# The first stage of a six-stage decoder kernel: decays beside the convolution, halves of the products added on GpSimd, root scale and out projection per step inside the mixing loop

## The chip, the cores and the metric

The kernel runs on one core of one Trainium2 chip. The time is the device time of one launch in microseconds (us). The kernel before takes 1787.82 us (median of 3 runs, 1786.68 to 1789.52). Engines are named as in the profile: PE is TensorE (PEld its weight loads), DVE is VectorE, ACT is ScalarE, POOL is GpSimd, SP is SyncE.

## What is computed

Two decoder layers over x of 8 sequences x 128 positions x 512 features. The change is in the first of six stages alone. That stage is a bottleneck of 512 to 128 features, two passes through one "hydra" block (a two-way state space mixer that runs over the 8 sequences as its time axis, with the 128 positions as batch), and the way back up:

```
hidden = gelu(x @ w_down.T + b_down)
for each of 2 layers:                       # u starts as hidden
    zxbcdt = u @ in_w.T                     # z 256 | xBC 288 | dt 8
    xBC = silu(causal_conv(xBC, 7 taps) + conv_b);  xs, B, C = split(xBC)
    dt_fw, dt_bw = softplus(dt + dt_bias)
    y = scan forward (shifted by one) + scan backward (shifted by one)
    y = y + xs * (xs @ fcD_w.T + D)
    yz = y * silu(z)
    u = (yz * rsqrt(mean(yz^2) + 1e-5) * norm_w) @ out_w.T
x = layernorm(2 x + up(mix of u and hidden) ...)
```

The scan over 8 steps is not run step by step. It is written as an 8 x 8 table of weights for each position and each of 4 heads, so that y of step t is the sum over the 8 source steps s of weight(t, s) times xs(s). Everything is float32.

## The kernel before, in words

All of it is written out by hand: each engine has its own program in `hydra_stage`, and semaphores order them. What stands first in an engine's program runs first there. A position is a partition (128), a step t is one of the 8 sequences (`L` = 8).

The stage begins with the loads, the down projection on PE (L256) and Gelu on ACT (L325). The context for the next stage is loaded into the same buffer as soon as the down projection has read it (L210), and POOL splits it in high and low parts in eight instructions, `cT_hi` and `cT_lo` (L243, L245). Then each layer goes through five parts, in a loop of two rounds on every engine:

1. z and convolution: for each t one matmul for z and dt (L268), then 1 to 7 taps of two passes each for the convolution (L275). ACT takes z out (L336, L337), DVE adds the bias (L382), ACT does Silu (L339).
2. Transposes of xs (L284) and the skip weights (L289) on PE. Beside them a chain of small instructions on DVE: softplus (L386 to L400), the sums of dt over distances (L405, L407), the exponents (L408, L411), Exp on ACT (L347), and the table of mixing weights `mixw` (L414 to L435).
3. The mixing loop: for each t DVE forms `prod` = xs times weight for all 8 sources (L442, 128 x 2048), PE adds the 8 sources with 8 matmuls by the identity (L298), DVE multiplies by silu(z) into `yz` (L448), ACT takes the square sum (L352). `prod` has two buffers.
4. After the loop, for all t together: the mean square (L450), its power of -1/2 on POOL (`rms`, L248), the scaling of `yz` (L453).
5. Transposes of `yz` (L306), the copy to `yT` with norm_w as scale (L356), the out projection with 512 columns (L311), and the copy to `uT` (L360), on which the next layer's first matmul waits.

At the end DVE forms `xtok` = 2 x + b_up (L456), the mix with the hidden (L461, L462), PE the up projection (L319), and DVE adds (L466).

## Time and profile before

| | |
|---|---|
| median of 3 runs | 1787.82 us |
| profiled execution, its own time | 1786.91 us |
| span of the trace in it | 1785.1 us |
| first stage, from the start to the last `xtok` addition | 204.6 us of the span |
| PE busy | 1564.1 us (88%) |
| DVE busy | 961.3 us (54%) |
| ACT busy | 769.7 us (43%) |
| POOL busy | 696.7 us (39%) |
| granted clock of PE, mean | 0.94 |

The busy shares are means over six stages that have different limits. For this change only the first 205 us count, and in them which engine waits for which, so the rows further down come from views of that stretch, and a few from a later stage where POOL and DVE work at the same time.

In a row of the timeline the two first numbers are the start and the duration in us, then come engine, line, operation, output<-input, the shapes, how many instructions the row merges, and in brackets the idle time before it with what ended it.

### The profile page before, as it was taken

To read this page: it belongs to the slowest core of one execution; us is meant where nothing else is said; L and a number is where in the kernel's file an instruction comes from. 1 tells how busy PE (TensorE), PEld (TensorE's weight loads), DVE (VectorE), ACT (ScalarE), POOL (GpSimd) and SP (SyncE) were. 2 spreads that over 40 slices of the span, in tenths; PEclk is the share of its full clock that TensorE was granted. 3 is DMA by queue.
4 is the path that set the end of the run, shared out by engine and by line. 5 is a ranking of instruction groups with operands and counts; after the bars stand their busy time and mean duration, and the time that the engine had idled before them with its cause. 6 is when DMAs were issued, how large, how long until landed. Compare 5 with 4: busy or idle time off the path is not lost. (4 is left out here: it accounts for less than half of the span.)

```text
span 1785.1 us, 28858 instructions
## 1 busy us (share of the span) xinstructions
PE 1564.1 (88%) x10647; PEld 1282.0 (72%) x10647; DVE 961.3 (54%) x1673; ACT 769.7 (43%) x2389; POOL 696.7 (39%) x561
## 2 busy tenths in 40 slices
PE   5888799999996789885899648999999999999846
PEld 3767597888885566665677437888888888888734
DVE  0627611333355889884466824555555555556644
ACT  2131223444443333332899824455455445445400
POOL 4100113443421455552533535555554555542210
PEclk9888899999998899997999878999999999999968
DMA  5100100100101342305000131101101110000011
GB/s 195 36 0 0 36 18 19 37 20 21 49 2 36 130 165 83 118 1 148 1 2 14 36 98 58 36 24 37 47 15 47 37 36 25 24 1 1 1 42 47
DMA packets 63475, 77.75 MB, mean 44 GB/s; under 512 B 13884, under 2 KB 43052, under 8 KB 63340
## 3 DMA queue, kind: packets, MB, share of 16 engines
q1 hardware_dynamic: 60860, 74.36, 13.2%
q8 instruction: 84, 1.38, 0.3%
q0 software_dynamic: 464, 1.32, 0.3%
q10 hardware_dynamic: 2016, 0.27, 0.1%
q14 instruction: 51, 0.42, 0.1%
HBM read 73.85 MB, written 2.10 MB: 43 GB/s over the span
## 5 line engine op out<-in xcount | busy, mean ns | idle before, releaser
L989 POOL TENSOR_TENSOR xa_rs<-xa_ms,minus_half 128x5 f32<-128x5 f32 x64 | 74.9, 1171 | 168.7 <-DVE xa_ms L1211 168.7
L1469 DVE SCALAR_TENSOR_TENSOR ff_acc<-ff_ring,ff_sT,ff_acc 128x512 f32<-128x512 f32 x168 | 125.5, 749 | 25.4 <-ACT ff_acc L1429 13.7
L972 POOL TENSOR_TENSOR xa_prob<-xa_prob,xa_inv 128x512 f32<-128x512 f32 x64 | 66.7, 1042 | 138.0 <-DVE xa_inv L1178 138.0
L1379 PE MATMUL ff_ring<-xT_hi,ff_w 128*128 128x512 f32 x224 | 96.5, 431 | 27.2 <-ACT ff_acc L1429 12.1
L1156 ACT ACTIVATE xa_prob<-xa_prob,xa_peak 128x128 f32<-128x128 f32 x256 | 99.8, 391 | 42.5 <-DVE xa_peak L1222 42.5
L1206 DVE TENSOR_REDUCE xa_ssq<-xa_qn 128x4 f32<-128x512 f32 x64 | 43.9, 686 | 135.2 <-ACT xa_qn L1142 135.2
L605 POOL TENSOR_TENSOR xa_prob<-xa_prob,xa_inv 128x1024 f32<-128x1024 f32 x32 | 60.7, 1897 | 142.2 <-DVE xa_inv L859 142.2
L71 PE MATMUL xa_qp<-xa_q_hi,xT_hi 128*128 128x512 f32 x256 | 107.4, 420 | 2.4 <-DVE xa_q_lo L1169 2.4
L71 PE MATMUL xa_rows<-xa_o_hi,xa_out_hi 128*128 128x512 f32 x256 | 102.6, 401 | 5.2 <-DVE xtok L1185 5.2
L1847 ACT ACTIVATE sa_work<-sa_work,sa_peak 128x128 f32<-128x128 f32 x256 | 99.2, 394 | 10.0 <-DVE sa_peak L1884 9.9
L73 PE MATMUL xa_rows<-xa_o_lo,xa_out_hi 128*128 128x512 f32 x256 | 102.9, 402 | 0.0
L72 PE MATMUL xa_rows<-xa_o_hi,xa_out_lo 128*128 128x512 f32 x256 | 102.6, 401 | 0.0
L72 PE MATMUL xa_qp<-xa_q_hi,xT_lo 128*128 128x512 f32 x256 | 101.9, 398 | 0.0
L73 PE MATMUL xa_qp<-xa_q_lo,xT_hi 128*128 128x512 f32 x256 | 101.4, 396 | 0.0
L841 DVE TENSOR_REDUCE xa_peak<-xa_score 128x4 f32<-128x1024 f32 x32 | 39.2, 1224 | 115.6 <-PE xa_score L683 115.6
L1142 ACT ACTIVATE xa_qn<-xa_qp 128x512 f32<-128x512 f32 x64 | 38.2, 597 | 141.6 <-PE xa_qp L73 141.6
L1681 POOL TENSOR_TENSOR sa_work<-sa_work,sa_inv 128x1024 f32<-128x1024 f32 x32 | 60.8, 1899 | 92.2 <-DVE sa_inv L1888 92.1
L1380 PE MATMUL ff_ring<-xT_lo,ff_w 128*128 128x512 f32 x224 | 91.7, 410 | 0.0
L71 PE MATMUL xa_kvp<-xa_kv_hi,cT_hi 128*128 128x256 f32 x256 | 78.2, 305 | 8.6 <-DVE xa_kv_lo L1164 8.6
L1379 PEld LDWEIGHTS ff_ring<-xT_hi,ff_w 128*128 128x128 f32 x224 | 44.2, 197 | 55.0 <-DVE ff_acc L1469 22.4
L73 PE MATMUL xa_kvp<-xa_kv_lo,cT_hi 128*128 128x256 f32 x256 | 72.5, 283 | 0.0
L72 PE MATMUL xa_kvp<-xa_kv_hi,cT_lo 128*128 128x256 f32 x256 | 72.5, 283 | 0.0
(389 smaller groups left out, 4786.5 us busy)
## 6 DMA issues: line engine op xcount, KB each, us to landing
xa_raw_q<-in_wq SPq DMA_DIRECT2D x8, 1024.0 KB, 5.5
xa_raw_o<-in_wo SPq DMA_DIRECT2D x8, 1024.0 KB, 5.4
ff_dn_q<-in_down_w SPq DMA_DIRECT2D x7, 512.0 KB, 3.7
ff_dn_z<-in_down_z SPq DMA_DIRECT2D x7, 512.0 KB, 4.7
ff_dn_s<-in_down_s SPq DMA_DIRECT2D x7, 512.0 KB, 6.4
pre<-in_wq SPq DMA_DIRECT2D x16, 192.0 KB, 3.2
pre<-in_wo SPq DMA_DIRECT2D x16, 192.0 KB, 4.0
sa_work<-in_w_qkvT SPq DMA_DIRECT2D x3, 1024.0 KB, 8.6
```

Source lines behind the costliest of these rows:

```text
L71: pe.matmul(out, a_hi, b_hi, start=first, stop=False)
L72: pe.matmul(out, a_lo, b_hi, start=False, stop=False)
L73: return pe.matmul(out, a_hi, b_lo, start=False, stop=last)
L605: pool.tensor_tensor(prob[:, t % 3, :, :], prob[:, t % 3, :, :], bc(inv[:, t % 3, :], 2, [P, Q, KEYS]), ALU.mult).then_inc(s["norm"], 1)
L972: pool.tensor_tensor(prob[:, u % 2, :, :], prob[:, u % 2, :, :], bc(inv[:, u % 2, :], 2, [P, Q, S]), ALU.mult).then_inc(s["norm"], 1)
L989: pool.tensor_tensor(rs[:, :], ms[:, :], m.minus_half[:, 0:Q + 1], ALU.pow).then_inc(s["rs"], 1)
L1156: last = act.activation(prob[:, u % 2, h, :], prob[:, u % 2, h, :], ACT.Exp, bias=peak[:, u % 2, h:h + 1], accum_out=total[:, u % 2, h:h + 1])
L1379: pe.matmul(bank[:, :], w[:, g % 2, c, a, f], m.xT_hi[:, c, cols], start=True, stop=False)
L1380: pe.matmul(bank[:, :], w[:, g % 2, c, a, f], m.xT_lo[:, c, cols], start=False, stop=True).then_inc(s["grp"], 1)
L1469: dve.scalar_tensor_tensor(acc[:, n % 2, i // 4, :], ring[(8 * n + i) % RING][:, :], column(n, i), acc[:, n % 2, i // 4, :], ALU.mult, ALU ...
L1681: pool.tensor_tensor(prob[:, u % 3, :, :], prob[:, u % 3, :, :], bc(inv[:, u % 3, :], 2, [P, HC, S]), ALU.mult).then_inc(s["norm"], 1)
L1847: last = act.activation(prob[:, t % 3, h, :], prob[:, t % 3, h, :], ACT.Exp, bias=peak[:, t % 3, h:h + 1], accum_out=total[:, t % 3, h:h + 1])
```

## The change

- **Loads.** `w_down` and `b_down` are loaded first, x in two halves of 512 columns; the first half of the down projection waits for its half alone.
- **Layer 1 reads the Gelu output itself** (`x_mid`) and no copy of it.
- **Order of z and convolution.** All 8 z matmuls come first, then the convolutions, which have four banks instead of two; the transposes of xs and the skip weights are put between the convolutions of later steps.
- **Decays beside the convolution.** On DVE the softplus, the distances, the exponents and the multiplication by dt stand between the bias additions. `xtok` = 2 x + b_up moves there too, in layer 1.
- **Halves on GpSimd.** POOL adds the upper four sources of `prod` to the lower four, in place (128 x 1024), and PE adds four sources instead of eight. `prod` has three buffers.
- **Per step inside the mixing loop.** The mean square, the root on POOL (128 x 1), the transposes of `yz` (now not scaled), the out projection with positions as rows (128 columns), the scaling by `rms` when ACT takes that out, a transpose back and the copy to `uT` are done for each t. norm_w is multiplied into `w_out` once. The separate scaling of `yz` is gone.
- The loops over the two layers are written out. The multiplication of `x_mid` by the mix factor moves to the start of layer 2.

The core of the diff:

```diff
-        prod = [sb(f"prod{i}", [P, L, DIN]) for i in range(2)]
-        yz = sb("yz", [P, L, DIN])
+        PRODS, GATED = 3, 4
...
+        prod = [sb(f"prod{i}", [P, L, DIN]) for i in range(PRODS)]
+        yz = sb("yz", [P, GATED, DIN])
...
+                def halves(n, t):
+                    pool.wait_ge(s["prod"], n + 1)
+                    x = prod[n % PRODS]
+                    pool.tensor_tensor(x[:, 0:L // 2, :], x[:, 0:L // 2, :], x[:, L // 2:L, :], ALU.add).then_inc(s["half"], 1)
+
+                def root(n, t):
+                    pool.wait_ge(s["msq"], n + 1)
+                    pool.tensor_tensor(rms[:, t:t + 1], msq[:, t:t + 1], m.minus_half[:, 0:1], ALU.pow).then_inc(s["rms"], 1)
...
-                with pool.Fori(0, LAYERS) as i:
-                    pool.wait_ge(s["msq"], i + 1)
-                    pool.tensor_tensor(rms[:, :], msq[:, :], m.minus_half[:, 0:L], ALU.pow).then_inc(s["rms"], 1)
+                for i in range(LAYERS):
+                    for t in range(L + 3):
+                        if t < L:
+                            halves(L * i + t, t)
+                        if t >= 3:
+                            root(L * i + t - 3, t - 3)
...
+                def mixed_sum(i, t):
+                    n = L * i + t
+                    pe.wait_ge(s["half"], n + 1)
+                    if t >= 2:
+                        pe.wait_ge(s["yz"], n - 1)
+                    for src in range(L // 2):
+                        last = pe.matmul(bank[2 + t % 2][:, 0:DIN], m.ident[:, :], prod[n % PRODS][:, src, :], start=src == 0, stop=src == L // 2 - 1)
+                    last.then_inc(s["y_mm"], 1)
...
+                    for t in range(L + 4):
+                        if t < L:
+                            mixed_sum(i, t)
+                        if 2 <= t < L + 2:
+                            turn_y(i, t - 2)
+                        if 3 <= t < L + 3:
+                            project_out(i, t - 3)
+                        if t >= 4:
+                            turn_u(i, t - 4)
...
+                    softplus_in(i)
+                    conv_bias(i, 0)
+                    conv_bias(i, 1)
+                    softplus_out(i)
+                    conv_bias(i, 2)
+                    conv_bias(i, 3)
+                    conv_bias(i, 4)
+                    distances()
+                    conv_bias(i, 5)
+                    exponents()
+                    if i == 0:
+                        dve.wait_ge(ld["up"], 48)
+                        dve.scalar_tensor_tensor(m.xtok[:, :, :], m.xtok[:, :, :], 2.0, bc(b_up[:, :], 1, [P, B, D]),
+                                                 ALU.mult, ALU.add).then_inc(s["xres"], 1)
+                    conv_bias(i, 6)
+                    decays(i)
+                    conv_bias(i, 7)
+                    mixing_weights(i)
+                    for t in range(L + 3):
+                        if t < L:
+                            products(i, t)
+                        if 2 <= t < L + 2:
+                            gated(i, t - 2)
+                        if t >= 3:
+                            mean_square(i, t - 3)
```

Where instructions stand before and after, at three places. First POOL, from the last split of the context to the end of the stage, before (L245 is `cT_lo`, L248 the root for all 8 steps):

```order
L245 TENSOR_TENSOR cT_lo<-pre,cT_hi 128x1024
L246 UNCONDITIONAL_BRANCH
L246 ISA
L248 TENSOR_TENSOR hy_rms<-hy_msq,minus_half 128x8
L246 REGISTER_ALU
L246 COMPARE_AND_BRANCH
```

and of the change, the first layer (L261 is `cT_lo`, L230 the addition of the halves, L234 the root of one step):

```order
L261 TENSOR_TENSOR cT_lo<-pre,cT_hi 128x1024
L230 TENSOR_TENSOR hy_prod<-hy_prod 128x1024 x4
L234 TENSOR_TENSOR hy_rms<-hy_msq,minus_half 128x1
L230 TENSOR_TENSOR hy_prod<-hy_prod 128x1024
L234 TENSOR_TENSOR hy_rms<-hy_msq,minus_half 128x1
L230 TENSOR_TENSOR hy_prod<-hy_prod 128x1024
```

POOL, which had one instruction per layer here, has sixteen, and none of them can start before its eight instructions for the context are done.

Second DVE, at the end of the convolution of the first layer, before (L382 is the bias addition of step 7, L386 to L397 the begin of softplus, L63 counts a semaphore's value):

```order
L382 TENSOR_TENSOR hy_xbc<-hy_bank,hy_conv_b 128x288
L386 TENSOR_TENSOR hy_sp<-hy_dt_raw,hy_dt_bias 128x64
L63 ISA
L389 SCALAR_TENSOR_TENSOR hy_sp<-hy_sp 128x64
L390 REGISTER_ALU
L391 TENSOR_SCALAR hy_sp<-hy_sp 128x64
```

and of the change, the same instructions among the bias additions (L454):

```order
L458 TENSOR_TENSOR hy_sp<-hy_dt_raw,hy_dt_bias 128x64
L461 SCALAR_TENSOR_TENSOR hy_sp<-hy_sp 128x64
L454 TENSOR_TENSOR hy_xbc<-hy_bank,hy_conv_b 128x288 x2
L465 TENSOR_SCALAR hy_sp<-hy_sp 128x64
L466 RECIPROCAL hy_sp<-hy_sp 128x64
L467 TENSOR_TENSOR hy_sp<-hy_sp 128x64
L468 TENSOR_TENSOR hy_sp<-hy_sp 128x64
L469 TENSOR_SCALAR hy_sp<-hy_sp 128x64
L471 SCALAR_TENSOR_TENSOR hy_sp<-hy_sp 128x64 x6
L472 SCALAR_TENSOR_TENSOR hy_sp<-hy_sp 128x64
L473 TENSOR_SCALAR hy_sp<-hy_sp 128x64
L474 SCALAR_TENSOR_TENSOR hy_dt<-hy_sp 128x64
```

The whole softplus now stands after the bias addition of step 1 and ahead of that of step 2 (the next row is L454 x3, steps 2 to 4).

Third DVE in the mixing loop, before (L442 products, L448 `yz`):

```order
L442 TENSOR_TENSOR hy_prod<-hy_xbc,hy_mixw 128x2048 x2
L448 TENSOR_TENSOR hy_yz<-hy_bank,hy_z_act 128x256
L442 TENSOR_TENSOR hy_prod<-hy_xbc,hy_mixw 128x2048
L448 TENSOR_TENSOR hy_yz<-hy_bank,hy_z_act 128x256
L442 TENSOR_TENSOR hy_prod<-hy_xbc,hy_mixw 128x2048
```

and of the change (L521 products, L532 `yz`, L536 the mean square of one step):

```order
L521 TENSOR_TENSOR hy_prod<-hy_xbc,hy_mixw 128x2048 x3
L532 TENSOR_TENSOR hy_yz<-hy_bank,hy_z_act 128x256
L521 TENSOR_TENSOR hy_prod<-hy_xbc,hy_mixw 128x2048
L532 TENSOR_TENSOR hy_yz<-hy_bank,hy_z_act 128x256
L536 TENSOR_SCALAR hy_msq<-hy_ssq 128x1
L521 TENSOR_TENSOR hy_prod<-hy_xbc,hy_mixw 128x2048
```

The products run one step further ahead of `yz`, and the mean square of each step is taken between them.

## Rows read from the trace of the kernel before

**Rows 1.** Windows: us, busy of PE, PEld, DVE, ACT, POOL, then PEclk, DMA, GB/s

```profile
53.20:70.30 17.10, 13.24 (x52) 11.54 (x53) 14.82 (x49) 3.25 (x9) 0.00 (x0) 0.50 0.27 91
70.30:97.00 26.70, 26.17 (x122) 22.69 (x120) 16.59 (x14) 3.60 (x15) 0.00 (x0) 1.00 0.00 1
101.00:111.20 10.20, 9.04 (x19) 4.08 (x20) 0.66 (x3) 4.52 (x15) 0.00 (x0) 0.50 0.00 0
111.20:138.50 27.30, 23.58 (x101) 17.70 (x99) 6.05 (x18) 11.46 (x34) 0.00 (x0) 1.00 0.00 0
```

**Rows 2.** Timeline of the mixing loop of the first layer, one step

```profile
79.24 0.42 DVE L448 TENSOR_TENSOR hy_yz<-hy_bank,hy_z_act 128x256 f32<-128x256 f32 x1 [0.83 <-PE hy_bank L298]
79.58 2.28 DVE L442 TENSOR_TENSOR hy_prod<-hy_xbc,hy_mixw 128x2048 f32<-128x2048 f32 x1
```

**Rows 3.** Timeline from the first layer's last square sum to the second layer's first matmul

```profile
97.76 1.68 POOL L248 TENSOR_TENSOR hy_rms<-hy_msq,minus_half 128x8 f32<-128x8 f32 x1 [45.73 <-DVE hy_msq L450]
99.47 2.19 DVE L453 TENSOR_SCALAR hy_yz<-hy_yz,hy_rms 128x256 f32<-128x256 f32 x8 [1.79 <-POOL hy_rms L248]
...
112.86 0.71 PE L268 MATMUL hy_bank<-hy_w_zdt,hy_uT 128*128 128x264 f32 x2 [0.69 <-ACT hy_uT L360]
```

**Rows 4.** Timeline before the loops: both layers' first products, the second layer's first `mixw` step

```profile
64.60 4.49 DVE L442 TENSOR_TENSOR hy_prod<-hy_xbc,hy_mixw 128x2048 f32<-128x2048 f32 x2
...
142.82 1.22 DVE L414 TENSOR_TENSOR hy_cb_prod<-hy_xbc 128x1024 f32<-128x1024 f32 x1
...
147.60 4.49 DVE L442 TENSOR_TENSOR hy_prod<-hy_xbc,hy_mixw 128x2048 f32<-128x2048 f32 x2
```

**Rows 5.** Timelines of POOL and DVE at four places where they meet

```profile
49.67 2.36 POOL L245 TENSOR_TENSOR cT_lo<-pre,cT_hi 128x1024 fp32r<-128x1024 f32 x1
50.52 0.46 DVE L382 TENSOR_TENSOR hy_xbc<-hy_bank,hy_conv_b 128x288 f32<-128x288 f32 x1 [3.38 <-PE hy_bank L275]
50.89 1.21 DVE L386 TENSOR_TENSOR hy_sp<-hy_dt_raw,hy_dt_bias 128x64 f32<-128x64 f32 x1
...
134.07 0.21 DVE L386 TENSOR_TENSOR hy_sp<-hy_dt_raw,hy_dt_bias 128x64 f32<-128x64 f32 x1
...
601.81 1.28 POOL L1337 TENSOR_TENSOR cT_lo<-ff_acc,cT_hi 128x512 fp32r<-128x512 f32 x1 [0.74 <-ACT cT_hi L1436]
601.92 1.72 DVE L1503 TENSOR_TENSOR ff_w<-ff_other 128x512 fp32r<-128x512 int32 x1
...
612.30 1.22 DVE L1476 TENSOR_TENSOR ff_dn_w<-ff_dn_q,ff_dn_z 128x1024 f32<-128x1024 int32 x1
612.53 2.15 POOL L1343 TENSOR_TENSOR ff_acc<-ff_acc 128x512 f32<-128x512 f32 x1 [3.06 <-DVE ff_acc L1469]
```

**Rows 6.** Lines, two of them: durations min/median/max in ns of DVE L1487 and POOL L1343

```profile
L1487 DVE TENSOR_TENSOR ff_w<-pre x4: 684/685/692, 574.0 to 575.8; 128x512 fp32r<-128x512 int32 x4
...
L1343 POOL TENSOR_TENSOR ff_acc<-ff_acc x28: 1281/1301/2146, 590.8 to 796.2; 128x512 f32<-128x512 f32 x28
```

**Rows 7.** Groups by line and shape, POOL, whole span: busy us, mean ns of one

```profile
L1546 POOL TENSOR_TENSOR rstd<-var,minus_half 128x1 f32<-128x1 f32 x32 | 19.2, 600 | 89.6 <-DVE var L1541 89.6
...
L245 POOL TENSOR_TENSOR cT_lo<-pre,cT_hi 128x1024 fp32r<-128x1024 f32 x4 | 9.4, 2357 | 0.3
```

**Rows 8.** Timeline of PE, first layer: a convolution of 7 taps and the skip weights

```profile
46.92 3.56 PE L275 MATMUL hy_bank<-hy_w_conv,hy_uT 128*128 128x288 f32 x14
...
56.77 6.83 PE L289 MATMUL hy_skip_bank<-hy_fcd,hy_xsT 128*128 128x4 f32 x32
```

**Rows 9.** Timeline: the down projection, w_conv, the first z, the context's split

```profile
17.01 9.83 PE L256 MATMUL hy_bank<-pre,hy_w_down 128*128 128x512 f32 x16 [17.01 <-DMA hy_b_down<-in_b_down]
17.67 4.44 POOL L239 TENSOR_TENSOR hy_w_conv<-hy_taps,hy_w_xbc 128x2016 f32<-128x2016 f32 x1 [9.44 <-DMA hy_w_xbc<-in_in_wT]
...
31.52 0.38 ACT L336 ACTIVATE hy_z_act<-hy_bank 128x256 f32<-128x256 f32 x1
...
34.83 1.89 POOL L243 TENSOR_TENSOR cT_hi<-pre,ones 128x1024 fp32r<-128x1024 f32 x1 [12.72 <-DMA pre<-in_ctxT]
```

More of the change, by code:

```diff
@@ new lines, in conv @@
+                def conv(i, t):
+                    u = uT if i else x_mid
+                    if t >= 4:
+                        pe.wait_ge(s["c_out"], L * i + t - 3)
+                    first = max(0, TAPS - 1 - t)
+                    for k in range(first, TAPS):
+                        last = pe.matmul(bank[2 + t % 4][:, 0:CONV], u[:, token(t - (TAPS - 1) + k)], w_conv[:, k, :],
+                                         start=k == first, stop=k == TAPS - 1)
+                    last.then_inc(s["c_mm"], 1)
@@ new lines, in turn_xs, with skip @@
+                def turn_xs(i, t):
+                    n = L * i + t
+                    pe.wait_ge(s["xbc"], n + 1)
+                    pe.wait_ge(s["z_out"], L * i + L)
+                    if t >= 2:
+                        pe.wait_ge(s["xs_T"], n - 1)
+                    for c in range(2):
+                        last = pe.transpose(bank[t % 2][:, c * P:(c + 1) * P], xbc[:, t, c * P:(c + 1) * P], m.ident[:, :])
+                    last.then_inc(s["xs_tr"], 1)
+                def skip(i, t):
+                    pe.wait_ge(s["xs_T"], L * i + t + 1)
+                    for c in range(2):
+                        last = pe.matmul(skip_bank[:, t * NH:(t + 1) * NH], xsT[:, c, token(t)], fcd[:, c, :], start=c == 0, stop=c == 1)
+                    last.then_inc(s["skip"], 1)
@@ new lines, in project_out, with turn_u @@
+                def project_out(i, t):
+                    n = L * i + t
+                    pe.wait_ge(s["y_T"], n + 1)
+                    if t >= 2:
+                        pe.wait_ge(s["u"], n - 1)
+                    for c in range(2):
+                        last = pe.matmul(bank[t % 2][:, 0:DM], yT[:, t % 2, c, :], w_out[:, c, :], start=c == 0, stop=c == 1)
+                    last.then_inc(s["o_mm"], 1)
+                def turn_u(i, t):
+                    n = L * i + t
+                    pe.wait_ge(s["o_out"], n + 1)
+                    pe.transpose(bank[t % 2][:, DM:2 * DM], u_tok[:, t % 2, :], m.ident[:, :]).then_inc(s["u_tr"], 1)
@@ L332, in _ @@
                 act.activation(neg_a[:, :], a_log[:, :], ACT.Exp).then_inc(s["a_exp"], 1)
-                with act.Fori(0, LAYERS) as i:
+                for i in range(LAYERS):
                     for t in range(L):
@@ new lines, in _ @@
+                        if t == 5:
+                            act.wait_ge(s["seg"], i + 1)
+                            act.activation(dec[:, :, :, :, :], dec[:, :, :, :, :], ACT.Exp).then_inc(s["dec"], 1)
+                        if t >= 2:
+                            out_xsT(i, t - 2)
+                    for t in range(L - 2, L):
+                        out_xsT(i, t)
+                    for t in range(2, L + 4):
+                        if t < L + 2:
+                            square(i, t - 2)
+                            out_yT(i, t - 2)
+                        if 3 <= t < L + 3:
+                            out_rows(i, t - 3)
+                        if t >= 4:
+                            out_uT(i, t - 4)
@@ new lines, in _ @@
+                dve.memset(seg[:, :, :, :, :], 0.0).then_inc(s["pool"], 1)
+                dve.wait_ge(ld["small"], 16 * 9)
+                dve.tensor_scalar(a_log[:, :], a_log[:, :], A_LOG_CEIL, None, ALU.min).then_inc(s["na"], 1)
+                for c in range(2):
+                    dve.tensor_scalar(w_out[:, c, :], w_out[:, c, :], norm_w[:, c:c + 1], None, ALU.mult).then_inc(s["w_out"], 1)
+                dve.wait_ge(s["alpha_exp"], 1)
+                pre = Chain(dve, s["alpha"])
+                pre.step(dve.tensor_scalar(sp[2][:, 0:1], sp[0][:, 0:1], 1.0, None, ALU.add))
```

263 lines of the change are left out of this document (130 added, 133 removed).

## The prediction, as it went on record before the changed kernel ran

> **What bounds the stage now.** I read the page first: PE is busy for 88% of the span, but that is a mean over six stages. So I took the windows of the first 205 us, then the timeline of that stretch, then groups by line and shape for prices, and last the timelines of POOL and DVE in a later stage, where both work at once.
>
> In the mixing loop PE is busy for 26.17 of 26.70 us at the full granted clock, 2.4 GHz [rows 1], and each step DVE waits 0.83 us for PE [rows 2]. A step takes 0.83 + 0.42 + 2.28 less an overlap of 0.08, 3.45 us, for 16 passes of PE: 0.216 us a pass. PE sets the loop.
>
> Outside the loop nothing is bound by an engine; it is a row of handovers. I cut the stage in five stretches. Start to the first product: 64.60 us. First product of layer 1 to the first matmul of layer 2: 64.60 to 112.86, 48.3 us [rows 3, 4]. Of this the loop takes 33.2 (to 97.76) and what stands behind it 15.1 (root 1.68, scaling 2.19, transposes, projection). From there to the second first product: 147.60 - 112.86 = 34.7 us. Layer 2's loop I take as the first one's, 48.3. The rest is the up projection, some 9 us.
>
> **Two things are taken from DVE's and POOL's rows before any sum.** Can they work at the same time? Layer 1 has the answer in one line: the addition of the dt bias (L386, two inputs in SBUF, 128 x 64) takes 0.21 us in layer 2 and 1.21 in layer 1, where it starts at 50.89 while POOL works on `cT_lo` from 49.67 to 52.03; it ends at 52.10, when POOL is done. The bias addition L382, one input of which is PSUM, takes 0.46 under the same POOL instruction [rows 5]. The later stage shows the same with large tiles: L1503 takes 1.72 us behind a POOL instruction of 1.28 and ends 0.55 after it, where the same shape takes 0.685 alone. The other way round POOL L1343 takes 2.15 instead of 1.28, and ends 1.16 after DVE's L1476 [rows 5, 6]. So a DVE instruction with two SBUF inputs and a POOL instruction wait for each other whole; only 0.12 to 0.14 us of start-up is hidden. The products (`xbc` and `mixw`, both SBUF) and the halves are just such a pair.
>
> The Trainium skill says the same (SBUF - State Buffer, section "Who interferes with whom"): DVE with two SBUF inputs and a GpSimd instruction that reads SBUF share one port pair, as a lock held for the full instruction. The trace agrees, but for the 0.13 us. By the page's rule taken to the letter a step below would be 5.24 us, by the rows 4.93.
>
> **The mixing loop, per step.** PE: 8 passes at 0.216 are 1.73; two transposes, the projection's four passes and the transpose back are seven passes of 128 columns or a weight load. Skip weights are such loads, 32 in 6.83 us at half clock (1.2 GHz), 0.213 each, so 0.107 at full [rows 1, 8]. PE needs 1.73 + 0.75 = 2.5 us at full clock, 4.95 at half. It is no longer the bound. DVE: 2.28 + 0.42 + 0.17 (mean square, as any tiny instruction) = 2.9. POOL: halves, two full inputs of 128 x 1024, as `cT_lo`, 2.36; root of 128 x 1 0.60 [rows 7]. The trace has no in-place addition of this size; L1343 is in place and half as large, 1.28, which gives the same slope.
>
> Now the lock. After the halves of one step the next product, which waited, takes the pair: 2.28 - 0.14 = 2.14. The root waits behind it and then needs some 0.40. The halves follow on POOL at once, 2.36 and 0.03, before DVE is back from `yz` and the mean square (0.65). Sum 2.14 + 0.40 + 0.03 + 2.36 = 4.93 us against 3.45 before. Eight steps are 39.4; only the first four roots come before the last halves, so 1.7 less: 37.7 us from the first product to the last half sum. Bounds: 8 x 4.5 if roots cost nothing, 39.5 if nothing of the start-up is hidden.
>
> Behind it: the sum on PE 1.8, `yz` 0.42, square 0.6, mean square 0.2, root 0.6, ACT's scaling 0.37, transpose 0.25, copy 0.37, and eight handovers of 0.1: 5.4 us at full clock. Between 97 and 101 the PE idles, and the clock then shows 0.50 until 111.2 [rows 1]; here PE idles in the same way, so the sum may take 3.5: 7.2. I take 6.1. Layer: 43.8 instead of 48.3, **-4.5 us, twice: -9**. (What is saved behind the loop, 9 us, is half eaten by 4.5 of a longer loop.) Range per layer -5.4 to -1.6.
>
> **Layer 2 up to the first product.** Before, the chain from L386 at 134.07 to L414 at 142.82, 8.8 us, and on to 147.60, 4.8, follows the last convolution [rows 4, 5]. After, the first 8.8 and the two multiplications by dt (0.8) stand beside convolutions of 20 us and are hidden there. But z comes first and is no longer hidden: two banks change hands between PE and ACT, some 0.65 us a step at full clock, 1.0 at half; I take 7.0 for eight, since the clock will have dropped in the tail. Convolution: 7 taps are 14 passes in 3.56 us less a drain of 0.15, 0.243 a pass [rows 8]; 35 taps are 17.0, with six transposes and four skips between them 20.0. Then bias 0.46, Silu 0.45, the table 4.0. Sum 31.9 against 34.7: **-2.8**. All at full clock -4.1; the convolution's begin at half clock too, which loses 2.9 (below), and z at 8, +0.9.
>
> **Layer 1 up to the first product.** The down projection waited until 17.01 for loads, and took 9.83 [rows 9]. With half of x first it can begin at about 8 to 10; I put its end at 17.5 to 19.8 instead of 26.8. The first z came out 4.7 us later (31.52), of which two copies of 0.6 fall away: now at 21 to 23.4. Eight steps of z, the first part of softplus and the Exp with its table: the long part of softplus starts at 28.5 to 30.7. The context's load is issued sooner too, but queues behind `xtok` and b_up; I put POOL's first `cT_hi` at 29.5 instead of 34.83 (27.8 if all of the seven are gained). POOL then works for 17.2 us in eight instructions without a gap.
>
> So softplus, 14 steps of which each but one waits on SBUF operands, runs under POOL. A step that waits for the pair gets in when a POOL instruction ends, is done in 0.2, and the next finds the pair taken: one step for each POOL instruction, as L386 did. Eight of 14 get through before POOL ends at 48; dt is ready at about 48.5 instead of 56.9. Behind the softplus on DVE is queued the bias addition of step 2, and for this waits PE: its transpose of step 0 to 2 and the convolution of step 5. PE stands from 35 to 50 and starts cold. What a cold start costs: the 16 passes of 512 columns of the down projection would take 6.9 us at 0.43 each and took 9.83 [rows 9], 2.9 lost. Convolutions 5 to 7 then take 6.3 + 4.1 + 3.8, and 5 us follow. First product at 66 to 69.5, take 67.6: **+3.0** against 64.60. `xtok`'s 4.4 us on DVE lie beside convolution 6. Bounds: -4 (softplus starts 2 us earlier than I think and POOL later), +5.5.
>
> The multiplication of `w_out`, the loops written out, the added table loads on ACT beside the convolution and the moved `x_mid` are put at nothing; ACT is busy for 11.46 of 27.3 us there [rows 1]. Last part: `hm` of the first half is ready before the last `uT`: **-0.5**.
>
> **Sum:** +3.0 - 9.0 - 2.8 - 0.5 = -9.3 us on the profiled execution's own time, 1786.91: 1777.6. That execution is 0.9 below the median, so I say 1778.
>
> **Rivals.**
> - *POOL and DVE work side by side in the loop.* Against it stand all of [rows 5]; for it only that the halves are in place. A step is then POOL's 2.96, say 3.05; a layer 2.3 + 24.4 + 5.4 = 32.1, -16.2 twice, softplus is free (-10), -2.8: 1741. 7%.
> - *Softplus gets through in layer 1* before POOL starts, or in the gaps between its instructions, and PE doesn't stand: layer 1 gains 8 instead of losing 3: 1767. For it: the order of these starts rests on loads that I estimate to 2 us. 13%.
> - *The clock stays at half* from the first wait on (slower). A mixing step needs 4.95 us of PE then, as much as the lock, and the two add up in part: 5.5 us. A layer is 51.2, +2.9 twice; layer 2's z and convolution +0.9, layer 1 +5.5: +12, 1799. For it: after every stretch of scattered PE work the clock shows 0.50 [rows 1]. Against: with PE busy for the whole of such a step it should rise again, as at 70.3. It decides from a step of 5.6 us up. 15%.
> - The forecast: 65%.
>
> **Numbers.** 0.2% is 3.6 us, about what a measurement of this kernel can tell from no change. The likeliest case alone reaches from 1767 (all lower bounds: -4, -5.4 twice, -4.1, -1) to 1790 (+5.5, -1.6 twice, +0.9). The range 1764 to 1792 takes in most of the second rival too and leaves out the first and most of the third. Faster: 0.5 of the 0.65, the first two rivals: 0.70. Within 0.2%: 0.13. Slower: 0.17.
>
> **What the profile would show.** Right: in the loop the products or the halves at 4.2 to 4.6 us mean duration by themselves (each holds the other's wait), a step of 4.8 to 5.2, PE under 60% busy there; softplus steps of 2 us in layer 1 under `cT_hi` and `cT_lo`, and a PE gap of over 10 us after convolution 4. Wrong: products at 2.28 and halves at 2.36 while they overlap; a first product of layer 1 well before 60 us; a clock of 0.50 through a whole loop.

## The result, and the profile after

The changed kernel takes **1784.68 us** (median of 20 runs, 1779.41 to 1786.81), the kernel before, run beside it, 1788.02 (20 runs). The ratio is 0.9976, 95% interval 0.9967 to 0.9985: 3.3 us faster by the medians, 2.7 to 5.9 by the interval. The direction and the range of the forecast hold, its size does not: -9.3 us were forecast.

The page of the kernel after, first its busy times, then one group (busy us, mean ns of one, idle before):

```profile
span 1782.6 us, 28716 instructions
...
PE 1543.3 (87%) x10583; PEld 1266.2 (71%) x10583; DVE 979.0 (55%) x1673; ACT 778.9 (44%) x2405; POOL 768.6 (43%) x591
...
L230 POOL TENSOR_TENSOR hy_prod<-hy_prod 128x1024 f32<-128x1024 f32 x16 | 57.7, 3622 | 59.4 <-DVE hy_prod L521 59.4
```

PE lost 21 us of work, the span only 2.5. POOL gained 72 us of busy time, of which the halves hold 57.7: 3.62 us each, though POOL needs 2.36 for a `cT_lo` of that shape [rows 7], 37.8 for sixteen. The other 20 us of the halves are waiting that counts as busy.

Windows of the kernel after, cut as the forecast cut them (columns as in [rows 1]): to the first product, loop, tail, layer 2 up to its product, loop, tail, up projection.

```profile
0.00:72.18 72.18, 40.72 (x150) 27.66 (x150) 32.17 (x68) 20.51 (x45) 28.16 (x27) 0.90 0.43 142
72.18:109.50 37.32, 24.42 (x85) 18.23 (x85) 26.80 (x20) 5.57 (x21) 34.95 (x13) 0.69 0.00 1
109.50:117.00 7.50, 5.75 (x36) 4.61 (x36) 1.77 (x6) 4.68 (x19) 2.44 (x4) 1.00 0.00 1
117.00:147.78 30.78, 27.44 (x135) 20.72 (x134) 14.20 (x57) 15.48 (x39) 0.00 (x0) 0.98 0.00 1
147.78:185.10 37.32, 24.17 (x86) 18.23 (x86) 26.94 (x20) 5.58 (x21) 34.95 (x13) 0.70 0.00 1
185.10:193.05 7.95, 6.21 (x37) 4.86 (x38) 1.58 (x5) 4.98 (x20) 2.56 (x4) 1.00 0.00 1
193.05:201.20 8.15, 7.27 (x16) 2.21 (x14) 6.15 (x9) 0.00 (x0) 0.00 (x0) 1.00 0.00 0
```

Against the stretches of before:

| stretch | before | after | measured | forecast |
|---|---|---|---|---|
| layer 1 up to the first product | 64.60 | 72.18 | **+7.6** | **+3.0** |
| layer 1, loop and tail | 48.3 | 44.8 | -3.5 | -4.5 |
| layer 2 up to its product | 34.7 | 30.8 | -3.9 | -2.8 |
| layer 2, loop and tail | 48.3 | 45.3 | -3.0 | -4.5 |
| from the last `uT` to the last addition | 8.7 | 8.15 | -0.5 | -0.5 |

The stretches sum to -3.3. The length of the loop itself is as forecast, 37.3 us twice, 37.7 said; so its row is off by the tail. What is most off is the first row. Timeline of the kernel after there:

```profile
14.72 9.83 PE L343 MATMUL hy_bank<-pre,hy_w_down 128*128 128x512 f32 x16 [14.72 <-DMA pre<-in_xT]
...
28.20 0.38 ACT L425 ACTIVATE hy_z_act<-hy_bank 128x256 f32<-128x256 f32 x1
...
32.52 1.89 POOL L259 TENSOR_TENSOR cT_hi<-pre,ones 128x1024 fp32r<-128x1024 f32 x1 [9.87 <-DMA pre<-in_ctxT]
...
37.58 1.17 DVE L465 TENSOR_SCALAR hy_sp<-hy_sp 128x64 f32<-128x64 f32 x1
...
38.78 0.55 DVE L466 RECIPROCAL hy_sp<-hy_sp 128x64 f32<-128x64 f32 x1
...
41.24 1.82 DVE L468 TENSOR_TENSOR hy_sp<-hy_sp 128x64 f32<-128x64 f32 x1
...
43.05 2.35 POOL L261 TENSOR_TENSOR cT_lo<-pre,cT_hi 128x1024 fp32r<-128x1024 f32 x1
43.09 2.36 DVE L469 TENSOR_SCALAR hy_sp<-hy_sp 128x64 f32<-128x64 f32 x1
...
45.48 5.30 DVE L471 SCALAR_TENSOR_TENSOR hy_sp<-hy_sp 128x64 f32<-128x64 f32 x6
47.33 2.34 POOL L261 TENSOR_TENSOR cT_lo<-pre,cT_hi 128x1024 fp32r<-128x1024 f32 x1
...
51.31 0.23 DVE L474 SCALAR_TENSOR_TENSOR hy_dt<-hy_sp 128x64 f32<-128x64 f32 x1
...
52.92 0.66 PE L298 MATMUL hy_bank<-ident,hy_xbc 128*128 128x128 f32 x2 [8.87 <-ACT hy_xsT L388]
...
54.08 4.96 PE L287 MATMUL hy_bank<-hy_w_conv,hy_x_mid 128*128 128x288 f32 x12
```

Read the durations of DVE's softplus steps: 1.82 and 2.36 us for what takes 0.2, each ending as a POOL instruction ends. PE stands for 8.87 us. Next in its program is the transpose of step 2's xs (L298), which needs the bias addition of step 2 on DVE and the Silu behind it, and DVE has that addition behind the softplus steps; the convolution of step 5 stands behind the transpose. (Its bank has been free since the bias additions of steps 0 and 1, at 37.7.) When that convolution starts, its 12 passes take 4.96 us, where a convolution of 14 takes 3.64 later. The reciprocal takes 0.55 under `cT_lo`, as it does in e2 with POOL idle: it did not wait.

### The profile page after: what moved, and what is told of

It reads as the page before. It is cut to its first block and busy times, and to the rows that moved or that the text cites. A ratio compares the mean times of both kernels' runs of the same rounds, so it can differ in the third digit from the quotient of the medians.

```text
span 1782.6 us, 28716 instructions
## 1 busy us (share of the span) xinstructions
PE 1543.3 (87%) x10583; PEld 1266.2 (71%) x10583; DVE 979.0 (55%) x1673; ACT 778.9 (44%) x2405; POOL 768.6 (43%) x591
## 5 line engine op out<-in xcount | busy, mean ns | idle before, releaser
L230 POOL TENSOR_TENSOR hy_prod<-hy_prod 128x1024 f32<-128x1024 f32 x16 | 57.7, 3622 | 59.4 <-DVE hy_prod L521 59.4
L1469 POOL TENSOR_TENSOR ff_acc<-ff_acc 128x512 f32<-128x512 f32 x28 | 41.3, 1474 | 76.3 <-DVE ff_acc L1595 76.3
```

## The experiments

Times are medians; "first" is the start of the first product of a layer, z2 the first matmul of layer 2, "up" the start of the up projection, all in the profiled execution. The ratio is to the kernel before, with its 95% interval. The five stages that follow are the same program in all these kernels. From "up" to the end of the trace it is 1585.3 us (e5) to 1593.0 (e6) in these executions (e10, whose up projection itself is longer, left out), 1590.0 in the changed kernel's. Why that differs was not looked into. So in a single profiled execution a few us are read more surely from the first stage than from the whole.

| kernel | us | ratio | first, layer 1 | z2 | first, layer 2 | up |
|---|---|---|---|---|---|---|
| before | 1788.0 | | 64.60 | 112.86 | 147.60 | 195.70 |
| after | 1784.7 | 0.9976 (0.9967-0.9985) | 72.18 | 116.99 | 147.78 | 192.57 |
| e1 eight on PE | 1775.2 | 0.9929 (0.9912-0.9947) | 72.57 | 113.26 | 144.06 | 184.84 |
| e2 split behind loop | 1779.7 | 0.9949 (0.9933-0.9965) | 58.62 | 103.42 | 139.99 | 184.78 |
| e3 product from PSUM | 1759.4 | 0.9835 (0.9817-0.9853) | 71.28 | 103.80 | 134.60 | 167.21 |
| e4 before + halves | 1808.1 | 1.0108 (1.0087-1.0129) | 64.36 | 122.44 | 157.19 | 214.39 |
| e5 = e1 + e2 | 1769.4 | 0.9896 (0.9875-0.9917) | 59.70 | 101.48 | 139.74 | 180.76 |
| e6 quarter, split behind | 1766.4 | 0.9878 (0.9857-0.9899) | 57.66 | 98.06 | 134.63 | 174.08 |
| e7 bias first, layer 1 | 1781.7 | 0.9960 (0.9949-0.9972) | 65.83 | 110.62 | 141.40 | 187.41 |
| e8 before + split behind | 1801.5 | 1.0079 (1.0058-1.0100) | 64.03 | 125.80 | 160.53 | 209.41 |
| e9 = e6 + bias first, layer 2 | 1767.5 | 0.9882 (0.9868-0.9897) | 58.90 | 98.79 | 133.35 | 173.72 |
| e10 quarter, split in gaps | 1766.7 | 0.9870 (0.9853-0.9886) | 59.92 | 98.67 | 129.46 | 172.51 |
| e11 second half of x waits | 1786.5 | 0.9993 (0.9981-1.0004) | 71.76 | 116.50 | 147.29 | 194.71 |
| e12 split in gaps, xtok kept | 1759.1 | 0.9835 (0.9821-0.9848) | 58.32 | 98.71 | 129.50 | 168.31 |

**e1: PE adds all eight sources.**

```diff
-                    pe.wait_ge(s["half"], n + 1)
+                    pe.wait_ge(s["prod"], n + 1)
-                    for src in range(L // 2):
+                    for src in range(L):
...
-                        if t < L:
-                            halves(L * i + t, t)
```

> The changed kernel with one part undone: PE adds all eight sources, POOL adds no halves. Theory A (the products on DVE and the halves on POOL wait for each other, 4.36 us a step and 4.9 with a root between): a step is now set by PE, 16 passes at 0.216 and 0.75 of transposes and projection, 4.2 us, the clock stays at full in the loop, products take 2.28 us each; first product to next layer's first matmul 39 to 41 us instead of 44.8; the kernel 7 to 11 us faster than the changed one, some 1775. Theory B (the halves help, the loop is long because of the clock and the handovers per step): PE has twice the passes, a step is 5 us or more, the kernel 5 us or more slower than the changed one.

1775.2: the halves alone cost 9.5 us by the medians, 8.4 by the two ratios. The loop of this kernel as a window (columns as above), and its products among the groups:

```profile
72.57:105.00 32.43, 30.08 (x145) 26.36 (x146) 21.34 (x20) 6.20 (x24) 10.69 (x5) 0.91 0.00 1
...
L519 DVE TENSOR_TENSOR hy_prod<-hy_xbc,hy_mixw 128x2048 f32<-128x2048 f32 x16 | 36.2, 2283 | 0.1
```

Products are back at 2.28 us, and PE, which has its full work again, sees a clock of 0.91 instead of 0.69. PE bounds this loop; that is cheaper than the lock.

**e2: the eight split instructions of POOL stand behind layer 1's mixing.**

```diff
-                pool.wait_ge(ld["ctx"], 16)
-                for c in range(KC):
...
+                for i in range(LAYERS):
...
+                    if i == 0:
+                        pool.wait_ge(ld["ctx"], 16)
+                        split(range(KC))
```

> The changed kernel; POOL's eight instructions that split the context stand behind layer 1's mixing loop, not ahead of it. Theory A (layer 1's first product is late, 72.2 us instead of 64.6, because softplus runs under these eight): softplus takes its 4 us, PE doesn't stand after the convolution of step 4, the first product comes at 58 to 60; of these 12 to 14 us some 4 are given back in layer 2, where the split now runs from 110 to 127 and meets the start of softplus; the kernel 8 to 10 us faster than the changed one, 1775. Theory B (layer 1 is late because z comes first and the loads and the first z came later than forecast): the first product stays within 2 us of 72.

Softplus and dt in layer 1, then in layer 2, where the split lies now:

```profile
36.67 1.52 DVE L475 SCALAR_TENSOR_TENSOR hy_sp<-hy_sp 128x64 f32<-128x64 f32 x6
38.71 0.22 DVE L478 SCALAR_TENSOR_TENSOR hy_dt<-hy_sp 128x64 f32<-128x64 f32 x1
...
58.62 8.84 DVE L525 TENSOR_TENSOR hy_prod<-hy_xbc,hy_mixw 128x2048 f32<-128x2048 f32 x3
...
116.76 2.40 DVE L472 TENSOR_TENSOR hy_sp<-hy_sp 128x64 f32<-128x64 f32 x1
```

The six L475, 5.30 us after, take 1.52; dt comes at 38.9 instead of 51.5, and the first product 13.6 us earlier. Layer 2 pays 5.8 of that back (z2 to first product 36.6 instead of 30.8), as softplus meets the split there. By the profile 7.8 us are left at the up projection; the median says 5.0, not the 8 to 10 expected (this profiled execution was the fastest of six, and its later stages took 1586.7).

**e3: the product reads its first input from PSUM.** The kernel leaves xs out of the product: a column of the skip bank stands in its place, so its output differs. All instructions keep their shapes.

```diff
-                                      xbc[:, :, 0:DIN].rearrange("p s (h n) -> p s h n", h=NH),
+                                      skip_bank[:, 0:1].unsqueeze(2).unsqueeze(3).to_broadcast([P, L, NH, HDIM]),
```

> The changed kernel, but the product reads one number of the skip bank (PSUM) in place of xs: same shape and type of output, one SBUF input left; xs is left out of the mixing, so the output is another. Theory A (it is the second SBUF input of the product that makes it and the halves wait): products and halves overlap, 2.3 and 2.36 us each, a step 3.0 to 3.2 us, a layer's loop part 32 to 34 us instead of 44.8, the kernel 20 to 24 us faster than the changed one, some 1762; layer 1's first product stays at 72. Theory B (POOL and DVE slow each other whatever DVE reads, or the loop is bound by the clock and handovers): step stays above 4 us and the time within 5 us of the changed kernel's.

POOL and DVE groups of this kernel:

```profile
L230 POOL TENSOR_TENSOR hy_prod<-hy_prod 128x1024 f32<-128x1024 f32 x16 | 37.4, 2350 | 63.2 <-DVE hy_prod L521 63.1
L521 DVE TENSOR_TENSOR hy_prod<-hy_skip_bank,hy_mixw 128x2048 f32<-128x2048 f32 x16 | 36.2, 2282 | 0.1
L234 POOL TENSOR_TENSOR hy_rms<-hy_msq,minus_half 128x1 f32<-128x1 f32 x16 | 9.6, 599 | 7.5 <-DVE hy_msq L536 7.5
```

With one SBUF input fewer on DVE, halves fall from 3.62 to 2.35 us, products from 3.02 to 2.28, roots from 1.11 to 0.60; the same instructions in the same order take 25.3 us less than in the changed kernel. A layer is 32.5 us (71.28 to 103.80), which is what the first rival had worked out for a loop without the lock (32.1). So the price of the lock in the loops is shown, not argued; a part of it goes through PE's clock, which shows 0.82 in this loop (71.28 to 97.50) and 0.69 in the changed kernel's. The product of e3 also reads one number where it read 2048. That this is not what sets the pair free is seen apart from e3: the bias additions read 288 numbers out of PSUM and keep 0.46 us under the split [rows 5].

**e4: the kernel before with the halves alone.** All else is as before.

```diff
+                    for t in range(L):
+                        x = prod[t % 2]
+                        pool.wait_ge(s["prod"], L * i + t + 1)
+                        pool.tensor_tensor(x[:, 0:L // 2, :], x[:, 0:L // 2, :], x[:, L // 2:L, :], ALU.add).then_inc(s["half"], 1)
...
-                        pe.wait_ge(s["prod"], L * i + t + 1)
+                        pe.wait_ge(s["half"], L * i + t + 1)
...
-                        for src in range(L):
+                        for src in range(L // 2):
```

> The kernel before with one part of the change alone: halves on POOL, four sources on PE, two product buffers as before. Theory A: a step goes from 3.45 to 4.4 us (2.14 + 2.23, the two wait for each other, and PE idles for half of it), the last yz of layer 1 comes at about 102 instead of 96.5; with the last sums at half clock 10 to 14 us slower in all, 1798 to 1802. Theory B (the halves take work from the bound engine and run beside the products): step 2.9 us, 8 to 10 us faster, 1778.

19 to 20 us slower, more than either theory gave. Timeline of one step:

```profile
86.76 2.34 POOL L250 TENSOR_TENSOR hy_prod<-hy_prod 128x1024 f32<-128x1024 f32 x1 [2.23 <-DVE hy_prod L446]
86.96 4.29 DVE L446 TENSOR_TENSOR hy_prod<-hy_xbc,hy_mixw 128x2048 f32<-128x2048 f32 x1
...
91.33 2.34 POOL L250 TENSOR_TENSOR hy_prod<-hy_prod 128x1024 f32<-128x1024 f32 x1 [2.23 <-DVE hy_prod L446]
```

A step is 4.57 us instead of 3.45, eight are 9 us, two layers 18. The clock from 64.36 to 105.00 is 0.71; the loop of before (64.60 to 97.80) has 0.91. The change as a whole earned back what its halves cost, and the halves were no part of the gain.

**e5: e1 and e2 together.**

> The changed kernel with both takings-back at once: PE sums all eight sources, and GpSimd splits the context behind the mixing loop of layer 1. Theory A (two separate losses by the pair of DVE and GpSimd: 9.5 us in the loops, 7.8 on the first stage by the split's place) has them add: up projection from about 177 us in the profile (192.6 after, 184.8 with either one alone), 1769 to 1771 us. Rival B (they are one loss seen twice, since what either frees is then waited for on PE) has about 1775 us, no better than the better one alone.

1769.4: in the time the two losses add (9.5 and 5.0 singly, 15.3 together). In the profile they do so only in part: the up projection starts at 180.76, not at 177. Against the single edits the first product is 1.1 us later, the first loop with its tail 1.1 longer and layer 2 up to its product 1.7 longer (38.3); why was not followed up.

**e6: as e5, but POOL adds a quarter.**

```diff
-                    pool.tensor_tensor(x[:, 0:L // 2, :], x[:, 0:L // 2, :], x[:, L // 2:L, :], ALU.add).then_inc(s["half"], 1)
+                    pool.tensor_tensor(x[:, 0:2, :], x[:, 0:2, :], x[:, 6:8, :], ALU.add).then_inc(s["half"], 1)
...
-                    for src in range(L // 2):
+                    for src in range(6):
```

> As the kernel with eight sources on PE and the split behind the loop, but GpSimd adds a quarter of the sources (128x512 onto 128x512) and PE sums six. Theory A (a step costs the larger of PE's own work and product plus GpSimd work, one after the other): PE some 3.7 us a step instead of 4.1, the pair 2.14 + 1.2 + 0.5 = 3.8 where a root is in the step; so 0 to 0.4 us a step are gained, 0 to 5 us in all: 1765 to 1771 us. Rival B (every GpSimd instruction that meets the products costs more than it takes from PE): slower than the kernel with all eight on PE by 3 us or more.

1766.4 (1764.3 to 1769.0) against 1769.4 (1765.6 to 1772.2). The medians are 3 us apart as theory A has it, and the up projection starts 6.7 us earlier, but the intervals of the two ratios overlap, so a gain of the quarter over none is likely and not shown in the time. Rival B is out. The first matmul of layer 2 in this kernel:

```profile
98.06 5.19 PE L283 MATMUL hy_bank<-hy_w_zdt,hy_uT 128*128 128x264 f32 x16
```

From it to layer 2's product are 36.6 us, as in e2, which has the split in the same place. The expectations of e9 and e10 measure against 34.9 and 35, which are too small.

**e7: in layer 1 three bias additions ahead of the long part of softplus.**

```diff
                     conv_bias(i, 1)
+                    if i == 0:
+                        for t in (2, 3, 4):
+                            conv_bias(i, t)
                     softplus_out(i)
```

> The changed kernel with one thing moved: in layer 1 DVE issues the bias additions of steps 2, 3 and 4 ahead of the long part of softplus; the context's split stays where it is, under softplus. Theory A (layer 1 is late because those additions, for which PE's convolutions 5 to 7 wait, stand behind softplus steps that get one turn for each GpSimd instruction): PE's convolutions don't stand, dt comes 1 to 2 us later than 51.5, the first product at 61 to 66 us instead of 72.2; 1775 to 1780 us. Rival B (the chain from dt to the weights alone decides): dt at 52 to 53.5 and the first product at 72 or later, 1785 us.

```profile
49.82 3.64 PE L287 MATMUL hy_bank<-hy_w_conv,hy_x_mid 128*128 128x288 f32 x14
...
51.47 0.23 DVE L474 SCALAR_TENSOR_TENSOR hy_dt<-hy_sp 128x64 f32<-128x64 f32 x1
...
65.83 8.84 DVE L521 TENSOR_TENSOR hy_prod<-hy_xbc,hy_mixw 128x2048 f32<-128x2048 f32 x3
```

dt is ready at 51.7, as in the changed kernel, but PE is by then at the convolution of step 6 and the first product starts 6.3 us earlier. (dt is late for another reason here: the long part of softplus starts at 46.24, behind the additions, and one of its steps, L467 with 1.84 us, still meets the split.) So of the 13.6 us between the changed kernel and e2, the queue behind softplus on DVE is worth 6.3; the other 7.2 are left as long as dt comes at 51.7. In time e7 gains 3 us (1781.7), less than the 5.2 at the up projection (of the 6.3, 1.2 go in a longer second loop) and short of the 1775 to 1780 expected: the mechanism is as theory A has it, its worth was put too high.

**e8: the kernel before with the split behind layer 1's mixing.**

```diff
                     pool.tensor_tensor(rms[:, :], msq[:, :], m.minus_half[:, 0:L], ALU.pow).then_inc(s["rms"], 1)
+                    if i == 0:
+                        pool.wait_ge(ld["ctx"], 16)
+                        split(range(KC))
```

> The kernel before with the context's split moved behind the first layer's mixing, nothing else. Theory A (before, the split lay beside bias additions that read PSUM and cost 1 us at most; the change brought softplus under it): first product at about 63.6 instead of 64.6, the split then lies beside layer 2's convolutions; 1786 to 1789 us, no difference that can be measured. Rival B (the split's place was a loss before too): 5 us or more faster, 1783 or less.

1801.5: both theories wrong, by a place that neither looked at.

```profile
100.27 1.88 POOL L243 TENSOR_TENSOR cT_hi<-pre,ones 128x1024 fp32r<-128x1024 f32 x1
100.32 17.36 DVE L457 TENSOR_SCALAR hy_yz<-hy_yz,hy_rms 128x256 f32<-128x256 f32 x8 [1.85 <-POOL hy_rms L249]
```

The eight scalings of `yz`, 2.19 us in [rows 3], meet the eight split instructions and get one turn for each: 17.36 us. Their operand is one tile in SBUF and a scalar per partition, so two SBUF tiles are no condition for the wait. The Trainium skill (SBUF - State Buffer, section "Who interferes with whom") names `tensor_scalar` among the operations that can take the shared pair, and `tensor_tensor` with two SBUF inputs apart from it; this row agrees, at 2.17 us a step. So the place that is good for the split in the changed kernel, where no scaling stands on DVE, costs the kernel before 13.6 us.

**e9: as e6, and in layer 2 (where e7 had it in layer 1) the bias additions of steps 2, 3 and 4 ahead of the long part of softplus** (`if i:` in the lines of e7).

> As e6 (quarter on GpSimd, split behind layer 1's mixing) with the order of the bias additions changed in layer 2, where the split now lies under softplus: steps 2, 3 and 4 ahead of the long part of softplus. Theory A (in layer 2 too, the additions queued behind stretched softplus steps make PE stand): layer 2 from z to the first product 31 to 33 us instead of 34.9; 1763 to 1765 us against 1766.4. Rival B (there the wait of PE is hidden by the chain behind dt): 34.5 us or more, no gain.

z2 to first product is 34.6 us instead of e6's 36.6. That is in rival B's range (34.5 or more), not in theory A's of 31 to 33, and 1767.5 is no gain. The queue behind softplus is worth 2.0 us there, not 6; why so little I did not follow up.

**e10: the split in four pieces, one behind softplus and one behind the exponents of each layer; xtok's doubling behind the last loop.**

```diff
+                    pool.wait_ge(s["chain"], 47 * i + 15)
+                    split((2 * i,))
+                    pool.wait_ge(s["seg"], i + 1)
+                    split((2 * i + 1,))
```

> Quarter on GpSimd as e6, and the context's split cut in four pieces of two instructions (4.3 us each), one behind softplus and one behind the exponents of each layer; xtok's doubling on DVE moves behind the last mixing loop. Theory A (what a stretch of GpSimd work costs is the number of small dependent DVE steps with SBUF operands that fall under it; of these pieces one or two distances each): first product of layer 1 at 57 to 60 us, layer 2 from z to the first product 31 to 33 us; the end 1 to 3 us longer for xtok; 1762 to 1766 us. Rival B (GpSimd's time itself is the price, wherever it stands): layer 2's stretch still 35 us, layer 1's first product 62 or later, 1770 us or more.

Layer 2 up to its product is 30.8 us (36.6 in e6), as in the changed kernel, which has no split there: theory A. The time, 1766.7, is just above its range and no better than e6's. The gain is lost at the end. Timeline:

```profile
166.92 4.42 DVE L589 SCALAR_TENSOR_TENSOR xtok<-xtok,hy_b_up 128x4096 f32<-128x4096 f32 x1
...
171.37 0.75 DVE L595 SCALAR_TENSOR_TENSOR hy_hm<-hy_uT,hy_mix,hy_x_mid 128x512 f32<-128x512 f32 x1
...
172.24 0.48 PE L344 MATMUL hy_bank<-ident,hy_u_tok 128*128 128x128 f32 x1 [3.48 <-ACT hy_u_tok L416]
172.51 10.14 PE L385 MATMUL hy_bank<-hy_w_up,hy_hm 128*128 128x512 f32 x16
```

The 4.42 us stand ahead of `hm` on DVE, PE idles for 3.48, and the up projection takes 10.14 instead of 7.90. Layer 2's product is 5.2 us earlier than in e6, the end of the up projection 0.7 later; the 1 to 3 us put down for `xtok` were too few.

**e11: the load of x's second half waits for the first.** 

```diff
                     sp_.dma_start(xT0[:, :, cols], io["xT"].rearrange("(c p) n -> p c n", p=P)[:, :, cols]).then_inc(ld[f"x{h}"], 16)
+                    if h == 0:
+                        sp_.wait_ge(ld["x0"], 16)
```

> The changed kernel, with the load of x's second half (and all of SP's loads behind it) issued only when the first half has landed. Theory A (both halves share the rate of the queues, so the down projection of the changed kernel starts at 14.7 and not at the 8 to 10 of the prediction because its first half lands with the second): start at 9 to 11.5 us, the second half lands 3 to 5 us behind it, dt and the first product of layer 1 move little, 1783 to 1787 us. Rival B (GpSimd's own loads, issued at the same time, or the way to the first landing set it): start still at 13 us or later, 1786 to 1792 us.

```profile
12.35 9.51 PE L345 MATMUL hy_bank<-pre,hy_w_down 128*128 128x512 f32 x16 [12.35 <-DMA pre<-in_xT]
```

The down projection starts 2.4 us earlier, and not at 9 to 11.5. The ten kernels that load as the changed one does started it at 13.04 (e6) to 15.59 (e5), so 12.35 is only 0.7 below what that spread gives. Neither theory is met, and how much of the 5 to 7 us by which I was off comes from the halves sharing the rate stays open; so does what holds the start at 12.35. The first product moves by 0.4 us, little, as expected (the second loop with its tail is 2.6 us longer than in the changed kernel, which nothing in the edit explains), and the time, 1786.5, can be told neither from before nor from after.

**e12: e10 with xtok's doubling back in layer 1; one piece of the split stands behind layer 1's mixing.**

```diff
                     split((2 * i,))
-                    pool.wait_ge(s["seg"], i + 1)
-                    split((2 * i + 1,))
+                    if i:
+                        pool.wait_ge(s["seg"], i + 1)
+                        split((3,))
...
+                    if i == 0:
+                        split((1,))
```

> As e10 (quarter on GpSimd, context's split in four pieces), but xtok's doubling is back where the changed kernel has it, beside the last convolutions of layer 1; the piece that stood there goes behind layer 1's mixing, into the 7 us before layer 2's softplus in which DVE has nothing to do. Theory A (e10 lost at the end, through xtok, what it won in layer 2): first product of layer 1 at 57 to 60 us, layer 2 from z to the first product 29 to 31 us, the end 8.6 us as in e6; 1761 to 1764 us. Rival B (the later stages take back what the first one gains): the same stretches of the first stage, and 1766 us or more.

1759.1 us, better than both theories' ranges, 30 us less than the kernel before in the same comparison (1789.2). Its stretches are as theory A has them: first product at 58.32, layer 2 up to its product 30.8, up projection 7.90 long. Rival B is out: the later stages took 1588.8 here. The same split, the same eight instructions:

```profile
97.22 1.89 POOL L259 TENSOR_TENSOR cT_hi<-pre,ones 128x1024 fp32r<-128x1024 f32 x1
...
98.71 5.19 PE L289 MATMUL hy_bank<-hy_w_zdt,hy_uT 128*128 128x264 f32 x16
...
99.19 2.35 POOL L261 TENSOR_TENSOR cT_lo<-pre,cT_hi 128x1024 fp32r<-128x1024 f32 x1
...
104.49 0.22 DVE L468 TENSOR_TENSOR hy_sp<-hy_dt_raw,hy_dt_bias 128x64 f32<-128x64 f32 x1 [7.13 <-ACT hy_dt_raw L436]
...
109.91 1.89 POOL L259 TENSOR_TENSOR cT_hi<-pre,ones 128x1024 fp32r<-128x1024 f32 x1 [8.37 <-DVE hy_dt L484]
111.88 2.36 POOL L261 TENSOR_TENSOR cT_lo<-pre,cT_hi 128x1024 fp32r<-128x1024 f32 x1
112.83 0.46 DVE L464 TENSOR_TENSOR hy_xbc<-hy_bank,hy_conv_b 128x288 f32<-128x288 f32 x1 [2.15 <-PE hy_bank L297]
113.20 1.07 DVE L490 TENSOR_TENSOR hy_seg<-hy_seg,hy_dt 128x24 f32<-128x24 f32 x1
```

A piece falls where DVE has nothing to do (7.13 us idle) or only bias additions out of PSUM (0.46, undisturbed); one distance waits 0.9 us (1.07), and further on the decays 1.3.

## Why the prediction was right or wrong, step by step

Forecast were -9.3 us, measured on the profile -3.3. The 6.0 between them are 4.6 in layer 1 up to the first product, 1.0 and 1.5 in the two loops with their tails, less 1.1 gained in layer 2.

- **Layer 1 up to the first product: +3.0 forecast, +7.6 measured. This is the step that failed.** Its mechanism was right, and rightly told: softplus under the split with one turn for each POOL instruction, the bias addition of step 2 queued behind it, PE standing, a cold start. Its size was not. The estimates that carried it were early: the down projection at 8 to 10 (14.72), the first z at 21 to 23.4 (28.20), the long part of softplus at 28.5 to 30.7 (37.58), and `cT_hi` at 29.5 (32.52). The first three are off by more than the last, so softplus starts 5 us behind the split and not with it. The split ends at 49.67 instead of 48, and seven of the 14 steps are still open then. My own count left six, and for them I had 0.5 us, room for two; they take 1.9. So dt at 51.5, not 48.5, is 3.0 of the 4.6 us. (The 48 was no sum either: 29.5 and 17.2 are 46.7.) From dt to the first product I said 19.1, it is 20.6: convolution 5 starts 2.5 us after dt, behind three bias additions, Silu and the transposes, a handover that I put at nothing, and what follows takes 18.1 instead of 19.2. e7 shows that the queue is worth 6.3 us of this stretch and e2 that the split's place is worth 13.6, almost twice the whole loss. How late the start is counts for little once the chain hangs on the split: the down projection starts 2.4 us earlier in e11 and the first product 0.4 earlier; it starts 0.8 later in e1 and the first product 0.4 later. The second rival was the same stretch without the split, -8 against before; e2 has -6.0.
- **The mixing loop: the lock right, the total in part by luck.** 37.7 us forecast, 37.3 measured, in both layers. The first four halves, with no root between them, take 4.36 us each; 4.53 were said. The four steps with a root were to take 4.93 each and take 4.37 on average, 17.5 together: two roots wait for a product and hold 2.60, two run in 0.55, and the last two halves (2.34, 2.35) meet no product, as DVE is ahead. Against that 2.2 us stand the 2.4 of the first product, before which no half can begin and which the sum left out. Of the signs that I named, the step of 4.8 to 5.2 us and PE under 60% busy did not come (4.4 and 65%), nor did a mean of 4.2 to 4.6 for products or halves (3.02 and 3.62); only the first four halves have it. By this timeline the pair alternates:

```profile
74.55 17.43 POOL L230 TENSOR_TENSOR hy_prod<-hy_prod 128x1024 f32<-128x1024 f32 x4 [24.88 <-DVE hy_prod L521]
78.92 3.78 PE L313 MATMUL hy_bank<-hy_prod,ident 128*128 128x256 f32 x8 [8.20 <-POOL hy_prod L230]
...
92.75 4.22 DVE L521 TENSOR_TENSOR hy_prod<-hy_xbc,hy_mixw 128x2048 f32<-128x2048 f32 x1
...
94.78 2.60 POOL L234 TENSOR_TENSOR hy_rms<-hy_msq,minus_half 128x1 f32<-128x1 f32 x1
...
107.11 2.35 POOL L230 TENSOR_TENSOR hy_prod<-hy_prod 128x1024 f32<-128x1024 f32 x1
```

- **The tail: 6.1 forecast, 7.5 and 8.0 measured.** I had summed the handovers of one step. Behind the last sum there are three rounds, 1.4 us each (PE's projections start at 112.89, 114.28 and 115.68), since every engine takes its queue in order; the last root takes 0.87 beside the multiplication of `x_mid`. Half clock was no part of it, it shows 1.00. This is argued from the timeline; no run took it apart.
- **Layer 2 up to the first product: -2.8 forecast, -3.9 measured,** near the bound of -4.1 that I gave for full clock; the clock shows 0.98 there. The eight z take 5.2 us and not 7.0. (By my own prices for z that bound is -4.6, and the lower bound of a layer's loop and tail, 36 and 5.4 against 48.3, is -6.9 and not -5.4; neither was reached.)
- **The end: -0.5, right.**
- **The rival that the clock stays at half** did not come as a whole, but in part: 0.69 in the loops, 0.50 in the first half of layer 1's (72.60 to 90.00), and full again in each tail. There a sum of eight passes takes 3.78 us, later 1.99, and the halves still come every 4.36.

What I missed in the sum as a whole: I took the halves as a part that pays (9 us saved behind the loop "half eaten" by a longer loop) and did not ask what the change would be without them. e1 says 1775.2.

## What to carry to other kernels

Before work is moved to GpSimd, list what DVE does at that time that reads SBUF. Where these are large instructions, as in the mixing loop, the two add up: 4.36 us for a pair of 2.28 and 2.35. Where they are small and depend on each other, the cost is not GpSimd's time but the number of DVE instructions under it, each of which takes as long as a GpSimd instruction, and whatever stands behind them in DVE's queue. The same eight instructions cost 13.6 us in layer 1 (after against e2), 5.8 in layer 2 (e2), and nearly nothing in four pieces (e12: 58.32, where e2 without a split has 58.62, and 30.8, where the changed kernel without one has 30.8); the best places are DVE's idle stretches and those in which it only reads PSUM. And a change made of parts is to be priced part by part: this one was worth 13 us without its halves.

## What the runs showed of the hardware that was not expected

- A DVE TENSOR_SCALAR with a single SBUF tile as input waits for GpSimd too: 2.17 us instead of 0.27 for 128 x 256 (e8), and 2.36 instead of 0.20 for L469 of the changed kernel. A reciprocal of one SBUF tile did not (0.55 in both).
- DVE and GpSimd take turns in all these rows, also when one has much less to do: a chain of tiny DVE steps gets one through between any two GpSimd instructions, and a GpSimd root of 0.55 us behind a product holds 2.60.
- With less work and longer waits PE's granted clock is lower: 0.91 in the loop of e1, 0.69 in that of the changed kernel. Of the work taken from PE a part came back in slower passes (eight in 3.78 us at first, 1.99 later). It is not the work alone: e3 gives PE as little as the changed kernel does, without the waits, and shows 0.82.
